# Scatters among the gathers in the last stage of a graph network, index lists made in two places, and scans one group later

## The reference, cut to what matters

```python
x = x + segment_sum(edge_weight[:, None] * (h @ W0)[dst], src) + bias        # layer 0: gathers at dst, sums at src
x = x + attention(h, src, dst)                # layer 1: softmax over the edges of each dst, sums at dst
x = x + hypergraph(h, src, dst, weight)       # layer 2: sums at min(dst, 19999), gathers back, sums at src
x = x + tensor_product(h, src, dst, edge_attr_4, edge_attr_8)   # layer 3: messages from src, sums at dst
# the weights of layer 3 are a small network on each edge:
w = silu(edge_attr_8 @ Wfc1 / sqrt(8)) @ Wfc2 / sqrt(64)
```

## Time and profile before

| | us |
|---|---|
| median of 3 runs | 3779.65 (3775.08 to 3782.87) |
| profiled execution, own time | 3784.34 |
| its span, first to last instruction | 3782.5 |
| busy: POOL | 2403.0 (64%) |
| busy: DVE | 2003.5 (53%) |
| busy: PE | 1933.2 (51%) |
| busy: ACT | 920.8 (24%) |

### The profile page before, as it was taken

One profiled execution on the slowest core, in us unless ns is written; L12 is line 12 of the kernel. 1 busy time (PEld: TensorE's weight loads), 2 busy tenths in 40 slices (PEclk: granted clock), 3 DMA queues, 4 the chain that ended last, 5 costly groups with the idle time before them and its releaser, 6 DMA issues.

```text
span 3782.5 us, 39731 instructions
## 1 busy us (share of the span) xinstructions
PE 1933.2 (51%) x8526; PEld 1456.1 (38%) x8526; DVE 2003.5 (53%) x6412; ACT 920.8 (24%) x2412; POOL 2403.0 (64%) x2088
## 2 busy tenths in 40 slices
PE   0000037777668689889363233666666466664000
PEld 0000025555644367777253222443333365563000
DVE  6964325555999655554786555222222299995000
ACT  0000024443000144544133444222222222221000
POOL 0767777788880477775003564788888754448887
PEclk9999987777999755555576555555555578886555
DMA  2999623355650132332377998666666544445443
GB/s 82 297 298 333 209 59 87 84 66 68 97 66 0 33 80 78 78 80 66 94 230 134 114 124 121 138 120 130 119 124 126 115 144 145 140 143 96 37 36 34
DMA packets 449411, 437.32 MB, mean 116 GB/s; under 512 B 77855, under 2 KB 359493, under 8 KB 449027
## 3 DMA queue, kind: packets, MB, share of 16 engines
q0 software_dynamic: 128576, 119.75, 26.0%
q1 hardware_dynamic: 280262, 283.65, 23.8%
q10 hardware_dynamic: 40512, 33.32, 3.6%
HBM read 262.12 MB, written 174.41 MB: 115 GB/s over the span
## 4 chain that ended last, share of the span: by engine, by line
POOL 21%; DVE 9%; issue 8%; DMA 7%; PE 2%; ACT 2%; DVEq 1%; SPq 0%; ACTq 0%; POOLq 0%
POOL out_dram L654 15%; POOL work L640 5%; DVE work L1668 3%; DMA he<-work 3%; DMA work<-flags_clip 1%; DMA work<-gat_h 1%; DVE big L1998 1%; DVE work L1654 1%; DVE work L1963 1%; DVE work L1966 1%; PE bank L829 1%; ACT work L1175 1%; DVE work L1644 0%; DMA out_dram<-big,idx_add_d 0%; PE bank L954 0%
## 5 line engine op out<-in xcount | busy, mean ns | idle before, releaser
L1668 DVE TENSOR_TENSOR_SCAN work<-work,bank 128x512 f32<-128x512 f32 (+1 forms) x343 | 426.5, 1265 | 462.4 <-PE bank L829 220.4
L640 POOL DMA_INDIRECT work<-d,idx_run_d x196 | 189.6, 967 | 379.0 <-DVEq L286 264.6
L829 PE MATMUL bank<-ident,work 128*128 128x128 f32 x588 | 151.3, 407 | 456.1 <-ACT work L1175 238.6
L1175 ACT ACTIVATE work<-work 128x128 f32<-128x128 f32 x784 | 317.4, 481 | 257.8 <-DVE work L1663 244.0
L654 POOL DMA_INDIRECT out_dram<-work,idx_add_s x196 | 311.4, 1589 | 60.2 <-issue 59.1
L654 POOL DMA_INDIRECT out_dram<-big,idx_add_s x196 | 308.8, 1575 | 62.6 <-issue 53.7
L654 POOL DMA_INDIRECT out_dram<-big,idx_add_d x196 | 306.7, 1565 | 59.7 <-issue 55.2
L640 POOL DMA_INDIRECT work<-s,idx_e_d x196 | 203.4, 1038 | 209.9 <-DVE work L1963 160.0
L707 POOL DMA_INDIRECT big<-out_dram,idx_src_d x196 | 195.6, 998 | 200.7 <-DVEq L286 141.2
L829 PEld LDWEIGHTS bank<-ident,work 128*128 128x128 f32 x588 | 98.5, 204 | 508.3 <-ACT work L1175 176.8
L640 POOL DMA_INDIRECT work<-rec_d,idx_e_s x196 | 218.0, 1112 | 77.7 <-issue 58.2
(11 more groups left out here) (324 smaller groups left out, 5283.2 us busy)
## 6 DMA issues: line engine op xcount, KB each, us to landing
out_dram<-big SPq DMA_DIRECT2D x71, 726.0 KB, 8.2
big<-in_x_dram SPq DMA_DIRECT2D x71, 704.0 KB, 7.0
work<-flags_src SPq DMA_DIRECT2D x98, 256.0 KB, 3.8
work<-flags_dst SPq DMA_DIRECT2D x98, 256.0 KB, 3.7
edge_w<-work SPq DMA_DIRECT2D x49, 512.0 KB, 3.7
work<-edge_w ACTq DMA_DIRECT2D x49, 512.0 KB, 3.6
gat_h<-work SPq DMA_DIRECT2D x49, 256.0 KB, 2.5
work<-gat_h SPq DMA_DIRECT2D x49, 256.0 KB, 4.2
```

Source lines behind the costliest of these rows:

```text
L640: g_.indirect_dma_start(to, None, table_ap, bass.IndirectOffsetOnAxis(ap=f[:, at_:at_ + 1], axis=0)).then_inc(of_rows(name).of(G), 16)
L829: last = T.transpose(out[:, t * P:(t + 1) * P], of[:, t * P:(t + 1) * P], ident[:, :])
L1175: last = S_.activation(h[:, t * P:(t + 1) * P], v(t), ACT.Relu, bias=stat[:, 8 + t:9 + t], scale=stat[:, t:t + 1])
L1668: return V.tensor_tensor_scan(to, flag_r[G.place][rows, :], of, before if G.from_(1) else 0.0, ALU.mult, ALU.add)
```

## The change

In stage 8, GpSimd issues after each group's gathers the scatters of the group six before. In stage 2, the placement of `last_col` is taken out of `onehots`; stage 7 makes it instead, with one buffer of one-hots (`hot_s`, `place_s`) and bank 7: VectorE writes them after widen(G), TensorE multiplies after net_out(G). `counts` keeps on VectorE only the reduction for equality; ScalarE takes the sum of sign(key - candidate) over the same PSUM columns, and "at most" follows from (signs + equals + 128) / 2. For this the banks of `rank` form a ring of four groups (all eight banks) instead of two, so TensorE waits until the first convolution is kept. In the first convolution the scans (and with them `delta`) run two groups behind `front`, and `keep` three.

The diff, cut to its core:

```diff
-            every_group(gathers("TP", s2_dram, [idx["sum_s"]], TP["taken"], D, in_r))
-            every_group(adds("TP", idx["add_d"], TP["kept"]))
+            take = gathers("TP", s2_dram, [idx["sum_s"]], TP["taken"], D, in_r)
+            add = adds("TP", idx["add_d"], TP["kept"])
+            late = 6
+            def body(G):
+                take(G)
+                if G.from_(late):
+                    add(group(G.g - late))
+            every_group(body)
+            for g in range(NG - late, NG):
+                add(group(g))
...
# TensorE, first convolution and rank
                 turn(G)
-                if G.from_(1):
-                    delta(G.before())
+                if G.from_(2):
+                    delta(G.before(2))
...
-                if G.from_(2):
-                    pe.wait_ge(MAPS["counted"], G.g - 1)
+                if G.from_(UNROLL):
+                    pe.wait_ge(MAPS["signed"], G.g - (UNROLL - 1))
...
-                    o = bank[2 * G.slot + t // 2][:, t % 2 * F:t % 2 * F + P + 1]
+                    o = bank[2 * G.place + t // 2][:, t % 2 * F:t % 2 * F + P + 1]
...
+            pe.wait_ge(GCN["kept"], NG)
             for_groups(pe, rank)
+            pe.wait_ge(MAPS["signed"], NG)
...
# TensorE, stage 7
+            def place(G):
+                pe.wait_ge(HYPSUM["onehot"], G.g + 1)
+                for t in range(GROUP):
+                    last = T.matmul(bank[7][:, 0:TILES], hot_s[:, t * P:(t + 1) * P], place_s[:, t * TILES:(t + 1) * TILES],
+                                    start=isinstance(G.g, int) and G.g == 0 and t == 0,
+                                    stop=isinstance(G.g, int) and G.g == NG - 1 and t == GROUP - 1)
+                last.then_inc(HYPSUM["placed"], 1)
...
                 net_out(G)
+                place(G)
...
# ScalarE
+            def signs(G):
+                if G.from_(1):
+                    act.wait_ge(MAPS["signed"], G.g)
+                act.wait_ge(MAPS["counted"], G.g + 1)
+                key, s = cols4(key_col["src"], G), cols4(n_sign, G)
+                for t in range(GROUP):
+                    last = S_.activation(junk[4 + t], bank[2 * G.place + t // 2][:, t % 2 * F:t % 2 * F + P], ACT.Sign,
+                                        bias=key[:, t:t + 1], scale=-1.0, accum_out=s[:, t:t + 1])
+                last.then_inc(MAPS["signed"], 1)
+            for_groups(act, signs)
...
# VectorE, stage 2
                 front(G)
-                if G.from_(1):
-                    chains(G.before())
+                if G.from_(2):
+                    chains(G.before(2))
                 scales(G, GCN, GROUP)
...
-                    for k, (c, op) in enumerate(((le, ALU.is_le), (eq, ALU.is_equal))):
-                        done(V.tensor_scalar(junk[2 * t + k], w, key[:, t:t + 1], None, op, ALU.add, accum_out=c[:, t:t + 1]))
+                    done(V.tensor_scalar(junk[t], w, key[:, t:t + 1], None, ALU.is_equal, ALU.add, accum_out=eq[:, t:t + 1]))
...
+            def onehot(G, hot, place, iota, row_c, col_c, of_c):
+                row, col, of = (cols4(c, G) for c in (row_c, col_c, of_c))
+                for t in range(GROUP):
+                    done(V.tensor_scalar(hot[:, t * P:(t + 1) * P], iota[:, 0:P], row[:, t:t + 1], None, ALU.is_equal))
+                    ins = V.tensor_scalar(place[:, t * TILES:(t + 1) * TILES], iota[:, 0:TILES], col[:, t:t + 1], of[:, t:t + 1],
+                                          ALU.is_equal, ALU.mult)
...
# VectorE, stage 7
+            link(...)   # six operations on 128 x 196: iota_s, row_s, col_s
             def body(G):
                 chain(G, HYPSUM, "HYPSUM", [bank[G.slot]], uT_r, "delta")
                 widen(G)
+                if G.from_(1):
+                    dve.wait_ge(HYPSUM["placed"], G.g)
+                onehot(G, hot_s, place_s, iota_s, row_s, col_s, last_col).then_inc(HYPSUM["onehot"], 1)
             for_groups(dve, body, order)
+            dve.wait_ge(HYPSUM["placed"], NG)
+            link(V.tensor_copy(idx["sum_s"][:, :], bank[7][:, 0:TILES]))
```

More of the change, by code:

```diff
@@ L312, in build_gnn @@
         GAT = loop_sems("gat", "var dev taken norm h hT hTs hh kept logits")
-        MAPS = loop_sems("maps", "step ranked counted onehot placed")
+        MAPS = loop_sems("maps", "step ranked counted signed onehot placed")
         GATSUM = loop_sems("gatsum", "h turned chained biased z delta kept")
         HYP = loop_sems("hyp", "var dev taken norm h turned chained he hes")
-        HYPSUM = loop_sems("hypsum", "turned chained delta kept at atT atTs fc fcs w ws wide")
+        HYPSUM = loop_sems("hypsum", "onehot placed turned chained delta kept at atT atTs fc fcs w ws wide")
         TP = loop_sems("tp", "taken var dev norm h hT hTs e feat turned chained delta kept")
@@ L366, in build_gnn @@
         iota_f = work[:, 10880:11136]
-        n_le, n_eq, n_blk, row_f, col_f, run_f, tmp_c = (work[:, 11136 + k * TILES:11136 + (k + 1) * TILES] for k in range(7))
-        place_r = ring(2400, GROUP * 2 * TILES)
+        n_sign, n_eq, n_blk, row_f, col_f, run_f, tmp_c = (work[:, 11136 + k * TILES:11136 + (k + 1) * TILES] for k in range(7))
+        place_r = ring(2400, GROUP * TILES)
         hot_r = ring(5536, 512)
+        place_s, hot_s = work[:, 3456:3456 + GROUP * TILES], work[:, 13712:14224]
+        iota_s, row_s, col_s = work[:, 4240:4240 + TILES], work[:, 13200:13200 + TILES], work[:, 13396:13396 + TILES]
         v8 = ring(2400, 1024)
@@ L859, in body @@
                 turn(G)
-                if G.from_(1):
-                    delta(G.before())
+                if G.from_(2):
+                    delta(G.before(2))
             for_groups(pe, body)
+            delta(group(NG - 2))
             delta(group(NG - 1))
@@ L880, in place @@
                 for t in range(GROUP):
-                    last = T.matmul(bank[4][:, 0:2 * TILES], hot_r[G.slot][:, t * P:(t + 1) * P],
-                                    place_r[G.slot][:, t * 2 * TILES:(t + 1) * 2 * TILES],
+                    last = T.matmul(bank[4][:, 0:TILES], hot_r[G.slot][:, t * P:(t + 1) * P],
+                                    place_r[G.slot][:, t * TILES:(t + 1) * TILES],
                                     start=isinstance(G.g, int) and G.g == 0 and t == 0,
@@ L1199, in body @@
                 norm(G, GCN, lambda t: v_r[G.slot][:, t * P:(t + 1) * P], h_r[G.slot], GROUP, small[G.slot])
-                if G.from_(2):
-                    keep(G.before(2))
+                if G.from_(3):
+                    keep(G.before(3))
             for_groups(act, body)
+            keep(group(NG - 3))
             keep(group(NG - 2))
@@ L1709, in body @@
                 front(G)
-                if G.from_(1):
-                    chains(G.before())
+                if G.from_(2):
+                    chains(G.before(2))
                 scales(G, GCN, GROUP)
             for_groups(dve, body, order)
+            chains(group(NG - 2))
             chains(group(NG - 1))
@@ L1731, in _ @@
             link(V.tensor_copy(col_f, to_int(tmp_c)))
-            link(V.tensor_scalar(to_int(n_le), pos[:, 0:TILES], F - 1, None, ALU.bitwise_and))
-            link(V.tensor_copy(iota_f[:, 0:TILES], to_int(n_le)))
+            link(V.tensor_scalar(to_int(n_eq), pos[:, 0:TILES], F - 1, None, ALU.bitwise_and))
+            link(V.tensor_copy(iota_f[:, 0:TILES], to_int(n_eq)))
             def steps(G):
@@ L1745, in counts @@
                 need(order.off)
-                key, le, eq, blk = (cols4(c, G) for c in (key_col["src"], n_le, n_eq, n_blk))
+                key, eq, blk = (cols4(c, G) for c in (key_col["src"], n_eq, n_blk))
                 for t in range(GROUP):
-                    w = bank[2 * G.slot + t // 2][:, t % 2 * F:t % 2 * F + P]
-                    for k, (c, op) in enumerate(((le, ALU.is_le), (eq, ALU.is_equal))):
-                        done(V.tensor_scalar(junk[2 * t + k], w, key[:, t:t + 1], None, op, ALU.add, accum_out=c[:, t:t + 1]))
+                    w = bank[2 * G.place + t // 2][:, t % 2 * F:t % 2 * F + P]
+                    done(V.tensor_scalar(junk[t], w, key[:, t:t + 1], None, ALU.is_equal, ALU.add, accum_out=eq[:, t:t + 1]))
                 for k in range(2):
-                    ins = V.tensor_copy(blk[:, 2 * k:2 * k + 2], bank[2 * G.slot + k][:, P:2 * F:F])
+                    ins = V.tensor_copy(blk[:, 2 * k:2 * k + 2], bank[2 * G.place + k][:, P:2 * F:F])
                     if k == 0:
@@ L1764, in _ @@
             need(order.off)
-            link(V.tensor_scalar(run_f, n_blk, float(P), float(-P - 1 - EP), ALU.mult, ALU.add))
-            link(V.tensor_tensor(run_f, run_f, n_le, ALU.add))
+            dve.wait_ge(MAPS["signed"], NG)
+            link(V.tensor_tensor(n_sign, n_sign, n_eq, ALU.add))
+            link(V.tensor_scalar(n_sign, n_sign, 0.5, float(P // 2 - P - 1 - EP), ALU.mult, ALU.add))
+            link(V.scalar_tensor_tensor(run_f, n_blk, float(P), n_sign, ALU.mult, ALU.add))
```

(10 more changed lines are left out.)

7 lines of the change are left out of this document (added).

## The result

The changed kernel takes 3540.72 us, the median of 4 runs (3537.82 to 3545.36); the kernel before, on the same chip, 3780.40 (3775.08 to 3782.87, 4 runs). The ratio is 0.9369, with a 95% interval of 0.9353 to 0.9385. The forecast was 3616, its range began at 3570: the kernel is faster than the range allowed. The profiled execution took 3545.4 us (span 3543.5), 239 us of span less than before.

What follows compares the result with a forecast made beforehand. It took one resource at a time as the bound: VectorE's lists ending stage 2, GpSimd in stage 7. 3784.3 - 137 + 120 - 147 = 3620.3, at the median's level 3616; 8-in-10 range 3570 to 3668.

Steps and rivals of the forecast that it cites:

- Stage 7, the step that failed: Stage 7: the moved list makes a ring of three engines the bound, 14.9 us a group, costing 120 us.
- The low end that I gave for the step: Stage 7: 13.3 us a group, for which the prediction wrote a cost of 45 us.
- Rival A: Stage 7 stays GpSimd-bound at 12.8 us a group through overlap or full TensorE clock; cost 10, total 3506; chance 0.12.
- Stage 2: Stage 2 gains 137 us, until GpSimd's last scatter sets the end; 60 if all three low gains came.
- VectorE's path: Stage 2: shortens by 89 + 42 + 50 = 181 us, ending at about 1090, with 44 us hidden.
- Rival B: Stage 2 gains only 60 to 110 us: TensorE's clock falls, ScalarE's sums cost twice; total about 3660; chance 0.10.
- Counting: Stage 2: four of eight reductions go to ScalarE, a group falls from 3.26 to 2.4 us, gaining 42 us.
- The one-hot lists: Stage 2: without the second list a group falls from 3.12 to 2.1 us, gaining 50 us, 10 at the half clock.
- Stage 8: Stage 8: scatters fill GpSimd's 160.0 us wait for VectorE, gaining 147 us, from 125 to 160.
- D: Rival: in stage 8 gathers and scatters close a ring and take turns, 21.2 us a group, total about 4020; chance 0.03.
- E: Rival: in stage 8 GpSimd's wait moves to kept, half the gain is lost, total about 3690; chance 0.05.
- C: Rival: stage 7 longer still, scatters stretching widen and one-hots, 15.6 to 16.2 us a group, about 3665; chance 0.07.

Runs made afterwards that it cites:

- e1: Changed kernel with stage 7's placement matmuls replaced by 11 transposes a group, both lists made in stage 2: 3528.21 us, ratio 0.9281 to the kernel before.
- e2: Changed kernel with stage 7's placement matmuls one group later on TensorE: 3515.30 us, ratio 0.9250 to the kernel before.
- e3: Changed kernel with both lists placed in stage 2 again and no placement in stage 7: 3505.66 us, ratio 0.9229 to the kernel before.
- e5: Changed kernel, both lists in stage 2; in stage 7 one-hots written twice, TensorE waits without multiplying; second chip kind: 3984.77 us, ratio 0.9505 to kernel before.

## Why the forecast missed

**Stage 7, the step that failed:** the 14.9 us a group has all of TensorE's pieces at the granted clock that the stage had before the change, 0.50. The mechanism was right: the place in the queue, the wait for the one-hots, GpSimd idle behind ScalarE (60.2 us), and at the half clock 14.83 us a group against 14.9. But I took the clock as a property of the stage, when in these runs it follows what TensorE is given to do. With the placements in it, it changed level within groups (0.50 and 0.98 in the late group above, 0.65 over the stage), and the mean period fell to 13.40. e1 and e2 show that the clock rises as much with another kind of work (0.67) or another place in the queue (0.66), e3 that it is back at 0.50 without the work, e5 that a wait alone does nothing. The term "a group 14.9" should have been 13.4, and 120 us becomes 47. No run shows its 2.75 us for the four matmuls of 196 columns, which was my estimate; the runs showed 2.98 us for them at 0.50, with the next transposes 2.77 us after their start in the first group. The low end that I gave for the step, 13.3 us a group, was next to the measured 13.4. (By the forecast's own sum it costs 42 us, not the 45 written there, and the far end, 15.6, 153 and not 154.) With 42 the whole comes to 3538. Yet the range began at 3570: the low end of the largest unknown term went into neither the range nor a rival.

**Rival A** named the rise of the clock and priced it only as a full return to GpSimd's 12.8 us (3506), with a chance of 0.12. The case between, a clock that rises for parts of a group, had neither chance nor price. I argued against A from 0.50 at 63% busy before; that says nothing of the same stage with more in it.

**Stage 2** came within 4 us of its term, since GpSimd's last scatter sets the end (1131.14 + 1.55 + 2.67 = 1135.36; forecast 1133.2). VectorE's path was mis-sized without cost, so that this term came out right by GpSimd's slack and not by its sizes: the path ends at 1040.2, not 1090, so 91 us are hidden and not 44. The first convolution gave nearly all of that: ScalarE's normalising runs from 525.2 to 926.0 before and from 522.7 to 787.0 after, 136 us less where the forecast had 89. The timeline around 640 us:

```profile
640.64 1.16 PE L852 MATMUL bank<-work 128*128 128x128 f32 x8
...
640.92 2.44 DVE L1705 TENSOR_TENSOR_SCAN work<-work,bank 1x512 f32<-1x512 f32 x2 [0.64 <-PE bank L866]
...
643.66 1.65 ACT L1199 ACTIVATE work<-work 128x128 f32<-128x128 f32 x4 [0.82 <-DVE work L1700]
...
645.40 1.13 PE L852 MATMUL bank<-work 128*128 128x128 f32 x8 [0.57 <-issue]
...
650.43 1.13 PE L852 MATMUL bank<-work 128*128 128x128 f32 x8 [0.87 <-issue]
```

A group takes 5.03 us here, some 5.5 over the stage (forecast 6.7). TensorE, its gaps closed, runs at a granted clock of 1.00 (640.64 to 655.50) where it had 0.68 in the group of the earlier trace rows (801.95 to 810.46). The turning matmuls take 1.13 us where they took up to 2.04. ScalarE waits 0.82 us for the scales and not 4.63. It is the error of stage 7 once more: I took TensorE's 6.67 us of work from a trace in which it stood idle in between. Rival B, a clock that falls as the gaps close, had the sign wrong: 0.73 before, 0.89 after.

Counting came close: 2.5 us a group, forecast 2.4. The groups by line show ScalarE's sum as two instructions:

```profile
L1239 ACT ACTIVATE work<-bank,key_src 128x128 f32<-128x128 f32 x196 | 69.4, 366 | 53.9 <-DVE work L1789 53.9
L1239 ACT ACTIVATION_READ_ACCUMULATOR work<-bank,key_src (+1 forms) x196 | 39.7, 202 | 0.0
```

The one-hot lists take 2.2 us a group, forecast 2.1. No run shows the 10 us that they were to gain at the half clock, a part of the low sum of 60 and my estimate: from 925 to 1035 us the clock was 0.95, and four matmuls of 196 columns took 1.59 us at 1.00 (L896, at 1000.80) where those of 392 columns took 2.90. But e3 shows that this edit gains nothing on the first kind of chip once the other two are in. I weighed it only by its share of a 181 us sum of which I knew that 44 were hidden. The right question was what the total is without the last edit: by my own numbers 181 - 50 = 131 of the 137 that GpSimd leaves to be gained, so 6 us against 120.

**Stage 8** gained 152.5 against 147. The first scatter goes out 36.8 us in (forecast 35), and all of the wait is gone, from the start-up and the end too. D and E are refuted: GpSimd waited 2.4 us in all for `kept` in this stage. C is refuted: no group of stage 7 took more than 14.83.

The scans' and the counting's own worth on the first kind of chip was not measured. An estimate from its rows: in e3 VectorE's last copy ends at 1120.3, and the next gather starts at 1137.4. Without the counting edit, 49 x (3.26 - 2.5) = 37 us more, it would end some 20 us behind that; without the scans' 136 us, some 120. What exactly makes the clock rise stays open too. On the first kind of chip the best version is the change without the moved list (e3), 3505.66 us; e2, with the list moved and placed one group later, is at 3515.30, and neither was run on the second kind.

## What to carry to other kernels

Price each edit of a bundle by taking it out of the finished whole: work that was moved away from a path with slack bought nothing and cost 46 us where it landed. Ask for which kind of chip the slack holds: on the other kind the same move was worth 60 us. When an edit adds work to TensorE or closes its gaps, price the stage at both clock levels seen, here 0.50 and 1.00, and let the range hold what lies between; durations read at the half clock need not hold for the changed kernel: the 2.07 us of net_out became 1.16 in the late group above. Before putting a wait into an in-order queue, try the place one group later: here it gave back all but 3 us.

## What the runs showed of the hardware

- The granted clock of stage 7 rose from 0.50 (before, e3) to 0.65, 0.66 and 0.67 (after, e2, e1) as 4 matmuls (up to 2.98 us) or 11 transposes (2.61 us) were added to each group, with or without a wait ahead of them; a wait of 7.01 us a group without the work left it at 0.50 (e5). Busy time alone doesn't tell the level: in stage 3 before, from 1500 to 1550 us, TensorE was busy 45.03 of 50 us at 0.50.
- A summing activation on ScalarE shows as two instructions, 0.366 and 0.202 us.
- Chips differ: with the same code, TensorE started one matmul every 2.80 us during GpSimd's gathers on one kind and was busy 199 of the same 250 us on the other, and the kernel before took some 4190 us and 3780 to 3798.
